# Last experts stage: gathers of the first part at set points of the second part's blocks, and a tile summed every third block

## The reference, cut to what matters

```python
h = _rms(x, ff_ln_w)
logits = h @ wg
topv, topi = jax.lax.top_k(logits, TOP_K)          # 4 of 16
gate = jax.nn.softmax(topv, -1)
a = jax.nn.silu(jnp.einsum('bsd,edh->bseh', h, w1)) * jnp.einsum('bsd,edh->bseh', h, w3)
y = jnp.einsum('bseh,ehd->bsed', a, w2)
moe = jnp.einsum('bsed,bse->bsd', y, weights)
return x + moe                                      # then x + tanh(g) * this
```

## Time and profile before

| | |
|---|---|
| median of 3 runs | 2604.84 us (2603.64 to 2608.91) |
| span of the profiled execution, first to last instruction | 2704.4 us |
| its own time outside the span | not recorded |
| PE busy | 2250.3 us, 83% of the span |
| DVE busy | 1841.5 us, 68% |
| ACT busy | 1152.8 us, 43% |
| POOL busy | 1105.8 us, 41% |

### The profile page before, as it was taken

One profiled execution on the slowest core, in us unless ns is written; L12 is line 12 of the kernel. 1 busy time (PEld: TensorE's weight loads), 2 busy tenths in 40 slices (PEclk: granted clock), 3 DMA queues, 4 the chain that ended last, 5 costly groups with the idle time before them and its releaser, 6 DMA issues. The chain is left out here.

```text
span 2704.4 us, 60407 instructions
## 1 busy us (share of the span) xinstructions
PE 2250.3 (83%) x20880; PEld 1699.7 (63%) x20880; DVE 1841.5 (68%) x3965; ACT 1152.8 (43%) x2509; POOL 1105.8 (41%) x1111
## 2 busy tenths in 40 slices
PE   6889989786878579994799899899888699998890
PEld 4555555443766357773677777787766577886670
DVE  4888888762547567775878878878876365444654
ACT  2777667554434223332344444444333354332230
POOL 2455555554144400001445445455577301325526
PEclk9898899765889689997999999999999799999995
DMA  5555455433358431211332332332334462445644
GB/s 115 125 134 141 121 137 131 113 114 100 104 178 277 133 130 52 64 31 51 82 83 62 81 85 59 81 87 57 85 100 135 134 206 90 142 148 167 200 153 144
DMA packets 249859, 313.10 MB, mean 116 GB/s; under 512 B 45152, under 2 KB 202848, under 8 KB 249056
## 3 DMA queue, kind: packets, MB, share of 16 engines
q1 hardware_dynamic: 188592, 219.11, 28.9%
q0 software_dynamic: 26624, 58.79, 7.9%
q10 hardware_dynamic: 34352, 31.34, 3.4%
HBM read 122.40 MB, written 102.24 MB: 83 GB/s over the span
## 5 line engine op out<-in xcount | busy, mean ns | idle before, releaser
L2119 POOL TENSOR_TENSOR ca_qk<-ca_qk,ca_q_swap 128x512 f32<-128x512 f32 x160 | 249.9, 1562 | 371.2 <-DVE ca_q_swap L2297 369.6
L735 DVE TENSOR_REDUCE soft_top<-soft_pa 128x2 fp32r<-128x512 f32 x512 | 328.4, 683 | 99.6 <-PE soft_pa L816 81.8
L630 ACT ACTIVATE soft_prob<-soft_pb 128x512 f32<-128x512 f32 x512 | 286.0, 594 | 191.8 <-PE soft_pb L809 171.9
L809 PE MATMUL soft_pb<-soft_rep 32*128 32x256 f32 x1024 | 213.4, 368 | 62.1 <-DVE soft_top L735 39.6
L809 PEld LDWEIGHTS soft_pb<-soft_rep 32*128 32x128 f32 x1024 | 140.1, 218 | 181.8 <-issue 85.8
L1440 PE MATMUL moe_pgu<-moe_w_hi,moe_xt_hi 128*128 x472 | 198.1, 420 | 39.8 <-DVE moe_xt_lo L1357 24.9
L816 PE MATMUL soft_pa<-soft_rep 31*128 31x256 f32 x1024 | 223.0, 375 | 6.0 <-DVE soft_top L735 3.5
L1459 PE MATMUL moe_py<-moe_w_d,moe_at 128*128 x788 | 219.1, 394 | 1.7 <-issue 0.8
L1363 DVE TENSOR_TENSOR moe_act_f<-moe_silu,moe_pgu 128x256 f32<-128x256 f32 (+1 forms) x236 | 88.5, 375 | 165.4 <-ACT moe_silu L1258 111.2
L2389 PE MATMUL ca_py<-ca_w_hi,ca_ot_hi 128*128 128x256 f32 x512 | 154.4, 302 | 33.1 <-DVE ca_ot_lo L2318 32.8
L1258 ACT ACTIVATE moe_silu<-moe_pgu 128x256 f32<-128x256 f32 (+1 forms) x236 | 82.1, 348 | 230.0 <-PE moe_pgu L1440 149.8
(11 more groups left out here) (377 smaller groups left out, 6384.7 us busy)
## 6 DMA issues: line engine op xcount, KB each, us to landing
ca_q_swap<-ca_q_f SPq DMA_DIRECT2D x640, 64.0 KB
moe_xs<-moe_rows SPq DMA_DIRECT2D x236, 128.0 KB
soft_rep<-soft_parts SPq DMA_DIRECT2D x378, 64.0 KB
moe_rows<-soft_blank SPq DMA_DIRECT2D x27, 768.0 KB
moe_ys_rows<-moe_ys ACTq DMA_DIRECT2D x134, 128.0 KB
moe_ys<-moe_ys ACTq DMA_DIRECT2D x102, 128.0 KB
moe_xd<-scratch SPq DMA_DIRECT2D x64, 128.0 KB
ca_vs<-ca_v SPq DMA_DIRECT2D x32, 256.0 KB
```

The lines of the kernel that those rows point to most:

```text
L630: act.activation(prob[:, k % 4, h, :], p_b[:, 2 * T * h:2 * T * (h + 1)], ACT.Exp).then_inc(prob_ready, 1)
L735: dve.tensor_reduce(heads[:, j, :, g], p_a[:, 2 * T * h:2 * T * (h + 1)].rearrange("p (c s) -> p c s", c=HALF), AX, ALU.max).then_inc(a_do ...
L809: mm = pe.matmul(p_b[:, out], rep[of, i % 4, g, at:at + PART], rep[of, i % 4, g, 0:T], start=True, stop=True)
L2119: pool.tensor_tensor(qk[:, u % 2, m, :], qk[:, u % 2, m, :], q_swap[:, p % 2, :], ALU.add).then_inc(qk_ready, 1)
```

## The change

The sums of part 0 begin every third loop step instead of every second (`EVERY`), from START[1] + 5 on instead of START[1] + 6. And each of part 0's gathers waits for a point of part 1's blocks. With T = START[1] + 3t these are: k = 0 for the copy of block T+1, k = 1 for act_f of block T+4, k = 2 for xt_lo of block T+6, k = 3 for xt_lo of block T+7. (A count of n on one of these semaphores is given by block n-1.) The first experts stage keeps its own order (`AHEAD`, `then`).

```diff
@@ -964,7 +964,7 @@
     KC = DIM // PART
     MC = HIDDEN // PART
     COUNT = MOE_TILES[name]
-    EVERY = 2
+    EVERY = 2 if then is not None else 3
     SUMS = 3 * KC // MC
@@ -1061,7 +1061,7 @@
         def combined_behind(b):
 
-            t, rest = divmod(b - START[1] - 6, EVERY)
+            t, rest = divmod(b - START[1] - (6 if AHEAD else 5), EVERY)
             return t if rest == 0 and 0 <= t < COUNT[0] and b < ALL else None
@@ -1189,6 +1189,14 @@
                     for k in range(TOP):
                         if AHEAD:
                             pool.wait_ge(y_ready, START[1] + TOP * t + k)
+                        elif k == 0:
+                            pool.wait_ge(y_ready, START[1] + EVERY * t + 2)
+                        elif k == 1:
+                            pool.wait_ge(act_ready, START[1] + EVERY * t + 5)
+                        elif k == 2:
+                            pool.wait_ge(xlo_ready, min(START[1] + EVERY * t + 7, ALL))
+                        else:
+                            pool.wait_ge(xlo_ready, min(START[1] + EVERY * t + 8, ALL))
                         gather(t, k)
```

## The result

The changed kernel takes 2682.44 us (median of 4 runs, 2676.45 to 2695.05), the kernel before 2604.24 on the same chip. The ratio is 1.0301, 95% interval 1.0259 to 1.0342: slower by 78 us. The forecast was slower by 43, with a range that ended at +58. The sign and both mechanisms were right. The price of the stall was not.

What follows compares the result with a forecast made beforehand. TensorE was taken to pace the last stage's blocks at 2.69 us each. Stall 36, plus queue end 12.4, less 5 given back, made +43 on 2604.84: 2648 us, range 2612 to 2663.

Steps and rivals of the forecast that it cites:

- both mechanisms: VectorE standing still for gather 3 once per tile, 36 us, and a later end of the gather queue, 12.4 us.
- stall, 20 tiles: In the block loop, VectorE's wait for gather 3 makes TensorE 1.8 us late per tile, 36 us; bounds 24 to 44.
- end of the queue: After the last block, tile 22's held gather and nine behind it delay tile 23's gather: +12.4 us, between 10 and 14.
- loss in the blocks given back: Breaking up the gather train regains time lost in the second part's blocks: 5 us taken, bounds 0 to 37.
- The stall, its steps: From the start of xt_lo: gather 3 at 1.20 us, first addition at 4.22, act_f at 4.61, next xt_lo at 6.07.
- Gather to addition 3.02: From the start of gather 3 on GpSimd to VectorE's first addition on its rows: 3.02 us.
- After, each comes alone, some 2 us apart: Part 0's gathers, before in a train 1.31 us apart and then in groups, would go out singly about 2 us apart.
- The cover: Delay TensorE tolerates: 1.65 us behind act_f and 1.57 behind xt_lo, leaving it 1.57 and 1.81 us late.
- The 37 us: Recorded loss over the second part's 63 blocks, 206.5 us against 169.5; about 5 us assumed present in timed runs.
- the heap of late reports: TensorE's finished work reported late and bunched to ScalarE's silu while gathers fly; taken as something holding up the recorded execution.
- Signs named ahead: Some 20 VectorE waits of about 3.4 us, copies in threes totalling 9.9 us, recorded stretch about 206 us again.
- rival 1: The 37 us are real in timed runs and pacing removes them: +11 us, 2616 us; chance 0.17.

Runs made afterwards that it cites:

- the new spacing: The changed kernel without the four waits on gathers: sums every third block, gathers free to run as buffers come free; 2615.85 us, ratio 1.0047.
- the one with seven buffers: The kernel before with seven tiles gathered early instead of three, using dead weights of experts 0 to 3 as buffers; 2589.55 us, ratio 0.9945.
- the kernel with both edits: The changed kernel with no points for gathers 0 to 2 and the sum's loads issued two blocks later; 2655.10 us, ratio 1.0190.
- the kernel with the stall alone: The kernel before plus one wait: gather 3 waits for the xt_lo directly ahead of its tile's first addition; 2655.07 us, ratio 1.0218.
- the three around it: The changed kernel without points for gathers 0 to 2 (2663.51 us), with the sum's loads two blocks later (2666.59 us), and with both (2655.10 us).
- half of the stalls: The changed kernel with even tiles' gather 3 waiting for xt_lo T+7 and only odd tiles' for T+8; 2673.02 us, ratio 1.0265.
- gathers 0 to 2 free: The changed kernel without the points of gathers 0, 1 and 2, gather 3 still waiting for its xt_lo; 2663.51 us, ratio 1.0222.

## Why the prediction went wrong, step by step

The two lengths add up to the measured times. From the copy of block 94 to the last addition the kernels take, by their traces: before, profiled again, 227.2; changed 304.0. The difference is 76.8, and 78 was measured.

| term | forecast | by the runs |
|---|---|---|
| stall, 20 tiles | 20 x 1.8 = 36 | 233.2 - 166.7 = 66.5, 3.3 per tile |
| end of the queue | 12.4 | 11.4 |
| loss in the blocks given back | -5 | -1 (167.9 without a stall before, 166.7 with the new spacing) |
| sum | 43 | 77 |

The stall's miss of 30 us is, per tile and times 20: 0.87 of landing, 17 us; 0.48 of clock, 10 us; 0.17 of cover, 3 us.

1. **The stall, its steps.** xt_lo to gather 1.20, measured 1.19. Addition to the next xt_lo 1.85, measured 1.86. "Gather to addition 3.02": right for a gather alone, 3.02 with both causes taken out; 3.89 in the changed kernel. **This is the term that was mis-sized.** The text took the landing from the last gather of before, behind which nothing follows and beside which no load runs, and bounded it with "I know of no row where it is longer once a gather is alone". That gather wasn't alone either: three stood ahead of it, 1.3 us apart, which by themselves don't lengthen a landing there (the last one of that train is 2.97 to 3.13 us in every kernel but the one with seven buffers). And the same trace had a longer one in the same train, 3.66, at tile 23:

```profile
2652.57 0.99 POOL L1179 DMA_INDIRECT moe_yg<-moe_ys,moe_held  x1 [0.30 <-issue]
2656.23 2.04 DVE L1331 SCALAR_TENSOR_TENSOR moe_xd<-moe_yg,moe_held,moe_xd 128x256 f32<-128x256 f32 x4 [4.31 <-DMA moe_yg<-moe_ys,moe_held]
```

In the changed kernel three gathers leave 1.9 to 6.1 us ahead of gather 3, because the stall itself drives the marks of gathers 0 to 2 together, and the loads of xd and sk are issued 1.0 and 0.7 ahead. "After, each comes alone, some 2 us apart" failed in the same way. The Trainium skill (DMA: Bandwidth & Descriptors, Anatomy of one DMA) gives an estimate of 2.3 us for such a transfer; no landing measured in these kernels was under 2.84, so the measurement decides against it.
2. **The cover.** 1.65 and 1.57 us behind VectorE's products, 1.8 as the price; the measured bearing of 2.25 puts it at 1.97 for the same wait, and 1.9 was measured in the kernel with both edits. Right within 4 us over 20 tiles.
3. **The clock** wasn't in the sum at all: 0.48 us per tile, 10 us. The text names no clock and gives no reason for leaving it out. Its falls stand behind stalls of 4.91 us and more in this kernel; with both causes of the long landing gone, no block runs at the lower clock, so here it follows from point 1. It isn't a rule of the stall's length: in the kernel with the stall alone it falls behind 4.24 us.
4. **The end of the queue**: 11.4 of 12.4, tile 23's gather 18.25 behind the copy of block 157 where 19.1 was forecast. Right.
5. **The 37 us**: taken as 5 in timed runs; by the second profile nothing of them is there, and the new spacing makes the stretch 1 us shorter. Reading the heap of late reports and the span of 2704.4 as an execution held up was right.
6. **Signs named ahead.** 20 waits of VectorE came, of 4.55 instead of 3.4 us; the copies go in threes, 6.86, 2.18 and 2.35 in the mean, 11.4 together instead of 9.9; the stretch is 233 instead of 206.

On 2604.24 the measured sum of 77 is 2681, and 2682.44 was measured: nothing of the difference is left over.

## What to carry to other kernels

- A point for a load, taken from an instruction directly ahead of the one that needs it, is a stall of one whole transfer. The price is the wait less what the blocks bear: 2.2 us more lead took 56 of the 66 us away here, another 3.0 the rest. Read the bearing from the steady rows before you place the point.
- A duration for a transfer is to be read where it will stand, with what is issued in the 5 us ahead of it. If the change itself delays something, follow the other marks through the delay: they come together.
- If one profiled execution is far longer than the timed runs (here 4%), profile it again before pricing what is lost in it. The second profile took the whole of rival 1 off the table.

## What the runs showed of the hardware

- The time from the start of gather 3, 128 KB, to the first use of its rows is 2.84 to 4.96 us in the changed kernel and the three around it, and up to 5.48 with half of the stalls. Three gathers in the 6 us ahead of it and two loads of 128 KB in the 1.3 us ahead account for 0.9 of it in the mean, shown by taking each away; either alone costs 0.3. In the changed kernel it is 3.21 where the nearest gather starts 3 us ahead and 4.16 where it starts 2 us ahead. Why tiles with the same issues at the same distances still differ by over 1 us (3.85 and 4.96) stays open.
- TensorE's clock fell to its lower level, 1.2 GHz, for about one block behind six of nine stalls of 5.21 us and more and one of 4.91 in the changed kernel, behind two of 4.94 and 5.19 us with gathers 0 to 2 free, and behind eight of 4.24 to 5.29 us in the kernel with the stall alone. Which of the stalls it follows is not settled. A block at the lower clock cost 1.3 to 1.4 us where TensorE paced (5.3 instead of 3.96 for two blocks) and nearly nothing where VectorE did.
- The same kernel took a span of 2704.4 us in one profiled execution and 2599.9 in another. In the longer one 39 us more lie in the stretch where gathers ran, with TensorE's reports up to 9 us late. Why that execution was held up isn't known; none of the other traces shows it.
